# Two depthwise convolutions in bands: row blocks of 38 rows copied as 32 and six, and bands laid out by rows

## The reference

```python
def _gn(v, G=32, eps=1e-5):
    B_, C_, H_, W_ = v.shape
    g = v.reshape(B_, G, C_ // G, H_, W_)
    m = jnp.mean(g, axis=(2, 3, 4), keepdims=True)
    s = jnp.var(g, axis=(2, 3, 4), keepdims=True)
    return ((g - m) / jnp.sqrt(s + eps)).reshape(v.shape)

x = x + _L0_conv_ref(_gn(x), L0_conv_k)        # depthwise 3x3, padding 1
x = x + _L1_conv_ref(_gn(x), L1_conv_weight)   # depthwise 7x7, padding 3, weight averaged over its four rotations
```

## Time and profile before

| | us |
|---|---|
| median of 3 runs | 3462.82 |
| lowest and highest | 3456.75, 3474.27 |
| the profiled execution's own time | 3465.62 |
| its span, first to last instruction | 3463.8 |

### The profile page before, as it was taken

One profiled execution on the slowest core, in us unless ns is written; L12 is line 12 of the kernel. 1 busy time (PEld: TensorE's weight loads), 2 busy tenths in 40 slices (PEclk: granted clock), 3 DMA queues, 4 the chain that ended last, 5 costly groups with the idle time before them and its releaser, 6 DMA issues.

```text
span 3463.8 us, 75946 instructions
## 1 busy us (share of the span) xinstructions
PE 2905.4 (84%) x28676; PEld 1702.8 (49%) x28676; DVE 2290.0 (66%) x4988; ACT 2185.6 (63%) x3969; POOL 1550.5 (45%) x1552
## 2 busy tenths in 40 slices
PE   0568888889888889989888988888988888898895
PEld 0235555455545555555454555555555555555453
DVE  3646666667666667666666666666766666767663
ACT  1436666667666667666666666666766666766672
POOL 3334444454444445444444444444444444544442
PEclk9889999999999999999999999999999999999998
DMA  7898899998889989898888898998989988988876
GB/s 123 193 239 246 253 256 258 254 255 250 254 249 257 251 254 259 252 256 256 249 252 249 249 254 252 258 253 253 251 254 256 255 251 251 262 255 259 249 224 191
DMA packets 1081095, 852.26 MB, mean 246 GB/s; under 512 B 204344, under 2 KB 990776, under 8 KB 1080664
## 3 DMA queue, kind: packets, MB, share of 16 engines
q1 hardware_dynamic: 675224, 646.03, 67.7%
q10 hardware_dynamic: 405504, 201.38, 20.4%
HBM read 262.32 MB, written 221.88 MB: 140 GB/s over the span
## 4 chain that ended last, share of the span: by engine, by line
PE 83%; issue 12%; SPq 3%; DVE 1%; DMA 1%
PE PS L685 43%; PE PS L713 39%; SPq L234 2%; PE PS L650 1%; PE PS L657 1%; DVE X L359 0%; DMA rows<-v_all 0%; SPq L225 0%; DMA v_all<-BT 0%; DMA BAND<-rows 0%; DMA BT<-H 0%; DVE X L479 0%; DMA v_all<-X 0%; DVE BT L374 0%; SPq L209 0%
## 5 line engine op out<-in xcount | busy, mean ns | idle before, releaser
L713 PE MATMUL PS<-BT,BAND 126*32 126x512 f16 x21504 | 1342.7, 410 | 436.5 <-issue 426.7
L685 PE MATMUL PS<-H,BAND 128*128 128x512 f16 x6912 | 1548.1, 383 | 61.2 <-DMA BAND<-rows 54.5
L614 POOL TENSOR_TENSOR H<-Z,H 128x512 f16<-128x512 f32 x768 | 846.5, 1103 | 1251.5 <-ACT Z L526 1250.2
L713 PEld LDWEIGHTS PS<-BT,BAND 126*32 126x32 f16 x21504 | 825.8, 133 | 949.2 <-issue 656.7
L685 PEld LDWEIGHTS PS<-H,BAND 128*128 128x128 f16 x6912 | 858.1, 126 | 700.4 <-DMA BAND<-rows 54.6
L606 POOL TENSOR_SCALAR H<-X,RB 128x512 f16<-128x512 f32 x768 | 679.0, 902 | 616.0 <-DVE RB L419 417.3
L523 ACT ACTIVATE H<-X,RB 128x512 f16<-128x512 f32 x768 | 618.0, 805 | 185.3 <-DVE H L452 175.8
L506 ACT ACTIVATE Z<-X,RB 128x512 f32<-128x512 f32 x768 | 561.3, 801 | 94.7 <-DVE RB L419 83.7
L526 ACT ACTIVATE Z<-X,RB 128x512 f32<-128x512 f32 x768 | 615.0, 801 | 0.0
L549 ACT ACTIVATE DUMP<-X 128x512 bf16<-128x512 f32 x768 | 479.7, 625 | 150.3 <-DVE X L479 150.0
L452 DVE TENSOR_TENSOR H<-Z,H 128x512 f16<-128x512 f32 x768 | 535.5, 752 | 47.4 <-POOL H L606 45.1
(11 more groups left out here) (45 smaller groups left out, 365.9 us busy)
## 6 DMA issues: line engine op xcount, KB each, us to landing
BT<-H SPq DMA_DIRECT2D x1152, 174.6 KB
X<-in_x SPq DMA_DIRECT2D x768, 256.0 KB, 4.2
out_y<-X ACTq DMA_DIRECT2D x768, 256.0 KB, 4.8
BT<-H SPq DMA_DIRECT2D x1152, 149.6 KB
BAND<-rows SPq DMA_DIRECT2D x96, 220.5 KB
rows<-v_all SPq DMA_DIRECT2D x8, 1764.0 KB, 11.5
BAND<-rows SPq DMA_DIRECT2D x192, 51.0 KB, 3.3
BAND<-rows SPq DMA_DIRECT2D x192, 49.5 KB, 3.8
```

The lines of the kernel that those rows point to most:

```text
L614: g.tensor_tensor(part(H1, n, 1, img, O1, P1), Z[:, img, :].rearrange("p (c w) -> p c w", c=CC), part(H1, n, 0, img, O1, P1), ALU.subtract ...
L685: last = mm(PA[:, ch, :], band[:, j, ws, :], data[:, :, O1 - 1 + j:O1 - 1 + j + W], start=k == 0, stop=k == 3 * K1 - 1)
L713: last = mm(banks2(n)[b * BL:(b + 1) * BL, ch, :], band[:, j, :], rows, start=j == 0, stop=j == K2 - 1, tile_position=(0, b * BL))
```

## The change

- Conv 2's blocks have 38 rows instead of 42, and 35 instead of 36 at the image's edge. `KW` becomes 114.
- Each block is copied by two transfers: its first 32 rows, and then its other six (three at the edge). A unit has 24 gathers: 12 of 32 rows, six of six, six of three. `gathered` counts up to twice as much (`LANDED`).
- `v1_all`, `rows1` and `BAND1` hold the four channels of a unit side by side within a row of the band, so that one partition's part of a transfer is one run of 1632 bytes (1584 at the edge) where it was four runs of 408 (396). The band that a conv 1 matmul reads from SBUF has 24 numbers between neighbouring columns where it had six.
- `rows2` has the band's row as its outermost dimension, so that one partition's part of a `BAND2` load is one run of 5376 bytes where it was 12 of 448.

```diff
-WIN = 42
-HALO = 5
-EDGE = 36
+WIN = 38
+HALO = 3
+EDGE = 35
...
-LANDED = 16 * TERMS * NB
+LANDED = 16 * TERMS * NB * 2
...
-    rows1 = nc.dram_tensor("rows1", (G * GC, Q, R1), F16, kind="Internal").ap()
-    rows2 = nc.dram_tensor("rows2", (G, 2 * GC, WIN, B2), F16, kind="Internal").ap()
...
+    rows1 = nc.dram_tensor("rows1", (G * CPU_, Q, CC * R1), F16, kind="Internal").ap()
+    rows2 = nc.dram_tensor("rows2", (WIN, G, 2 * GC * B2), F16, kind="Internal").ap()
...
-        BAND1 = sb("BAND1", [P, GC, B1], F16)
+        BAND1 = sb("BAND1", [P, CPU_, CC * B1], F16)
...
-                sp.dma_start(rows1[g0 * GC:g1 * GC],
-                             bass.AP(v1_all.tensor, g0 * GC * V1 + (Q - 1) * 2 * K1,
-                                     [[V1, (g1 - g0) * GC], [-2 * K1, Q], [1, R1]])).then_inc(rows1_cut[g0 > 0], 16)
+                sp.dma_start(rows1[g0 * CPU_:g1 * CPU_],
+                             bass.AP(v1_all.tensor, g0 * GC * V1 + (Q - 1) * CC * 2 * K1,
+                                     [[CC * V1, (g1 - g0) * CPU_], [-CC * 2 * K1, Q], [1, CC * R1]])
+                             ).then_inc(rows1_cut[g0 > 0], 16)
...
-                sp.dma_start(rows2[g0:g1].rearrange("g c r k -> (g c) r k"),
+                first = rows2[0:1, g0:g0 + 1, :]
+                sp.dma_start(bass.AP(rows2.tensor, first.offset,
+                                     [[B2, (g1 - g0) * 2 * GC], [G * 2 * GC * B2, WIN], [1, B2]]),
...
-                    first = TERMS * r0 + k
-                    sp.dma_start(BT[first:first + TERMS * (hi_row - lo_row - 1) + 1:TERMS, q, b, :, :],
-                                 H2[lo_row:hi_row, q, which, :, :]).then_inc(gathered[q], 16)
+                    for first, last in ((lo_row, lo_row + BL), (lo_row + BL, hi_row)):
+                        to = TERMS * (r0 + first - lo_row) + k
+                        sp.dma_start(BT[to:to + TERMS * (last - first - 1) + 1:TERMS, q, b, :, :],
+                                     H2[first:last, q, which, :, :]).then_inc(gathered[q], 16)
...
-                        k0 = (m0 - (q * Q - 1)) * 2 * K1
-                        sp.dma_start(BAND1[q * Q:(q + 1) * Q, c * CC:(c + 1) * CC, m0 * 2 * K1:m1 * 2 * K1],
-                                     rows1[bass.ds(g * GC + c * CC, CC), :, k0:k0 + (m1 - m0) * 2 * K1]
-                                     .rearrange("c r k -> r c k")).then_inc(band1_loaded[c], 16)
+                        k0 = (m0 - (q * Q - 1)) * CC * 2 * K1
+                        sp.dma_start(BAND1[q * Q:(q + 1) * Q, c, m0 * CC * 2 * K1:m1 * CC * 2 * K1],
+                                     rows1[g * CPU_ + c, :, k0:k0 + (m1 - m0) * CC * 2 * K1]
+                                     ).then_inc(band1_loaded[c], 16)
...
-                        sp.dma_start(BAND2[k:KW:TERMS, half, :, :],
-                                     rows2[bass.ds(g, 1), which * GC:(which + 1) * GC, :, :]
-                                     .rearrange("g c r k -> r (g c) k")).then_inc(band2_loaded[half], 16)
+                        sp.dma_start(BAND2[k:KW:TERMS, half, :, :].rearrange("r c k -> r (c k)"),
+                                     rows2[:, g, which * GC * B2:(which + 1) * GC * B2]
+                                     ).then_inc(band2_loaded[half], 16)
...
-                    band = BAND1[:, c * CC + ch, :].rearrange("p (m j s) -> p j s m", m=P, j=K1)
+                    band = BAND1[:, c, :].rearrange("p (m k j s) -> p k j s m", m=P, k=CC, j=K1)[:, ch]
```

More of the change, by code:

```diff
@@ L317, in _ @@
             done = [0, 0]
-            w1v = w1_t.rearrange("g (c i j) -> g c i j", c=GC, i=K1)
+            w1v = w1_t.rearrange("g (t c i j) -> g t c i j", t=CPU_, c=CC, i=K1)
             sq = lambda a: a.rearrange("g (c i j) -> g c i j", c=GC, i=K2)
-            v1v = v1_sb.rearrange("g (c p j s) -> g c p j s", c=GC, p=V1P, j=K1)
+            v1v = v1_sb.rearrange("g (t p c j s) -> g t p c j s", t=CPU_, p=V1P, c=CC, j=K1)
             v2v = v2_sb.rearrange("g (s c p j) -> g s c p j", s=2, c=GC, p=V2P)
@@ L366, in prepare @@
                 if layer == 0:
-                    rows = [(v1v[:, :, Q + 1 - dy, :, 0], v1v[:, :, Q + 1 - dy, :, 1], w1v[:, :, dy, :])
+                    rows = [(v1v[:, :, Q + 1 - dy, :, :, 0], v1v[:, :, Q + 1 - dy, :, :, 1], w1v[:, :, :, dy, :])
                             for dy in range(K1)]
                 else:
-                    rows = [(v2v[:, 0, :, WIN - K1 - dy, :], v2v[:, 1, :, WIN - K1 - dy, :], sq(wt)[:, :, dy, :])
+                    rows = [(v2v[:, 0, :, WIN + 2 - HALO - dy, :], v2v[:, 1, :, WIN + 2 - HALO - dy, :], sq(wt)[:, :, dy, :])
                             for dy in range(K2)]
```

## The result

| | before | changed |
|---|---|---|
| median, us | 3468.55 | 4610.32 |
| lowest, highest | 3456.75, 3475.05 | 4599.87, 4615.5 |
| profiled span | 3463.8 | 4605.1 |

The ratio is 1.328, 95% interval 1.324 to 1.331: the changed kernel is a third slower. Forecast were 3980 us and a range of 3640 to 4400.

The account below looks back on a forecast made before the run. Twelve full DMA engines were taken to bound the kernel at 17.07 us a unit. Engines 0 and 1 at 19.5 us add 455 us, the start 60: 515 over the profiled 3465.6 gives 3980 us, range 3640 to 4400.

Parts of the forecast that it names:

- The bound of before: Kernel before: gathers come late and hold the unit at 17.07 us, not PE with its 14.4 us.
- the twelve engines: Kernel before: twelve DMA engines, always the same lowest ones, are full to 99%, 16.9 of 17.07 us a unit.
- SP's issues: SP's queue: issuing 24 gathers, loads and bands takes 16.5 us a unit, hidden under the engines' 19.5 us.
- A large piece: SP's queue: issuing a gather of 32 rows on 16 engines costs 0.36 us, 12 a unit.
- Loads: SP's queue: issuing four loads a unit costs 0.55 us each, 2.2 us.
- the second rival: SP's queue bounds if 32 rows cost as much to issue as 42: 21.3 us a unit, 4315 us; chance 15%.
- The engines' sum: DMA engines 0 and 1: stores, loads, gathers and bands sum to 19.3 us, at 99% full 19.5 a unit.
- The row's price: Gathers on the DMA engines: each row costs 0.238 us with its share of signals.
- the first rival: Gather rows on engines 0 and 1 get cheaper as most engines are no longer full: 3625 or 3415 us; chance 15%.
- The start: Second cut for `rows1` on three engines instead of twelve: SP's next load is held longer, +60 us.
- weight loads: Conv 1 on PE: 126 ns under a matmul every 219; would have to grow by 90 ns to count.
- the share of the queues: The two DMA queues: share of 16 engines falls from 89% to about 75%, though the kernel is slower.

Follow-up runs that it names:

- before_half: Kernel before the change with every gather row half as long (two of four channels): 3199.4 us.
- one_transfer: Changed kernel with blocks of 38 and 35 rows each gathered in one transfer instead of two: 6308.5 us.
- bands_only: Changed kernel's band layout alone, with blocks of 42 and 36 rows gathered as before: 3473.2 us, ratio 1.0003 to the kernel before.
- experiment 9: bands_only with the cuts for `rows1` over 16 and 80 units instead of three and 93: 3415.1 us, ratio 0.985 to the kernel before.
- experiment 1: Changed kernel with the small gathers (six and three rows) still issued, but each row only 32 bytes: 4544.8 us.

## Why the prediction was wrong

**The bound of before: right in part.** That gathers, not PE, hold the unit is borne out by before_half, and that transfers use as many engines as the divisor says, always the same ones, by the packet counts and one_transfer. That the twelve engines are full to the last per cent was not shown: bands_only takes packets from them, and the unit goes from 17.1 to 17.0 us; a sum of packet times can also be 6% too large (experiment 9). And the prediction overlooked that SP had almost no slack before the change either. The two largest of its waits in the walk, in the view of the kernel before, are

```profile
SPq L184 <- POOL H L606: 71.3, 31, 9.4
SPq L253 <- PE PS L685: 27.8, 21, 2.0
```

and with its gathers' own waits they come to 112 us for all 192 units, 0.6 us of 17.1.

**The failed step: SP's issues, "16.5 us, under 19.5. Hidden, but with little to spare".** SP was occupied for all but 0.1 of the 23.0 us of a unit. Four things made that sum too small.
- A large piece: 0.36 us taken, 0.53 to 0.55 measured. I had taken it from two single transfers of 32 partitions between SBUF and device memory (0.33 and 0.40 us) that stood behind a quiet SP. 12 a unit: +2.1 us.
- The 0.04 us from one issue to the next stand in no term: 31 issues a unit, +1.3 us.
- What SP is held for. I summed least times, though the view of before had 16 us of issues in a unit of 17.1 whose least times sum to some 12, and I had read its slow issues as proof that the engines were full. Here 24 gathers take 17.7 us in the mean of five units, 16.2 by the single issues with 0.04 us each.
- Loads: 2.2 us taken, 4.25 in the mean of these five, since the one behind `BAND2` takes 10.3.

With bands it makes 23 us. With nothing held it would be 16.2 + 2.1 + 1.2 = 19.5, as much as the forecast gave the engines: the prices alone took SP from 16.5 to there (loads and small pieces come out 0.4 lower than I took them), and the holds the other 3.5 us. What a held issue waits for the profile doesn't name; behind `BAND2` and the cuts it is transfers on two or three engines, for the gathers it stays open. This is the second rival's result, SP as the bound, but not its condition (32 rows do cost less to issue than 42: 0.53 against 0.75 us), and above the 21.3 us that I gave it. It had 15% where it deserved most. I compared two sums, 19.5 and 16.5, as if the smaller were covered. But a serial queue has no cover of its own: every hold adds to it. **A sum of least times isn't a bound for a queue that is occupied for 16 of 17.1 us already.**

**The engines' sum, 19.5 us.** For it no run gives a value. `BAND2` did go to two engines and costs 200 us, half of the 2.4 us a unit that I had put on it, as a hold. The row's price, taken as fixed at 0.238, ranges from 0.18 (two and seven engines) to 0.30 us (sixteen, six and three): against the first rival's reasoning it is highest where most engines take part, though the queues are emptier than before. Small pieces don't explain it: with theirs all but empty (experiment 1) a row costs 0.29 by the same steps.

**The start.** +60 us taken, +18 measured (97.3 against 79.3). 992 runs of 1632 bytes on three engines took 72 us in all, 73 ns each; at 18 GB/s I had 122. The term was within its bounds, not at their middle.

**The rest** held: weight loads grew, and stay under the matmuls; the share of the queues fell, further than the 75% forecast, as the unit is longer; a slower clock is seen (granted 0.849 of full in the mean, 0.937 before; conv 2's matmuls 465 ns instead of 410) and costs nothing here: SP waited for PE 0.3 us in the whole walk.

## What to carry to other kernels

Count a change's transfers before its bytes: in these runs each piece cost its issuing queue 0.5 to 0.75 us whatever it carried, and the queue's own row in the trace, with its gaps, tells whether that is covered. A queue without gaps is a bound, and a transfer on few engines can hold what is issued behind it: three `BAND2` loads on two engines cost the next load 8.2 us, the cut on three engines 70. Where a count of rows sets the number of engines, look for the split that gives 16 in the one-off transfers at the start too: here that was worth 1.5%, more than any of the layouts.

## What was not expected of the hardware

- The price of a gather's issue on SP goes with the number of engines, though not in its order: 0.53 us on 16, 0.61 on four, 0.65 on eight, 0.70 on three, 0.70 to 0.76 on six, twelve and fourteen. The bytes have no part in it (0.70 and 0.76 us with rows of 32 bytes as with rows of 4256, experiment 1). Band loads from device memory on 16 engines cost less, 1.80 us for four.
- A row from SBUF to SBUF costs 0.18 us on few engines and 0.30 on sixteen, by packet times. Why, stays open: reading neighbouring partitions at one time explains it in small part at most.
- Runs of 1632 bytes from device memory to device memory take 73 ns each on three engines, against 54 ns for 408 bytes on twelve: four times the bytes for 1.35 times the time, though not with the same number of engines at work.
